# Transposes of softmax weights moved from the tensor engine to transposing DMAs in seven of eight attention passes

## The reference

```
q = heads(norm(x) @ Wq + bq);  k = heads(ctx @ Wk + bk);  v = heads(ctx @ Wv + bv)
attn = softmax(q k^T / sqrt(32))          # 128 x 2048 for each of 2 x 16 heads
out = (attn @ v) @ Wo + bo
```

## Time and profile before

| | us |
|---|---|
| median of 3 runs | 515.41 |
| the profiled execution | 515.1 |
| its span | 513.3 |
| PE busy | 495.2 |
| ACT busy | 266.2 |
| DVE busy | 307.7 |
| POOL busy | 42.2 |

### The profile page before, as it was taken

How to read it: one execution, slowest core, us unless ns; L and a number is a source line. 1 busy time by engine, 2 the same in 40 slices (tenths; PEclk the granted TensorE clock), 3 DMA queues, 4 the chain that set the end, 5 groups by cost and what they waited for, 6 DMA issues and landing times.

```text
span 513.3 us, 9255 instructions
## 1 busy us (share of the span) xinstructions
PE 495.2 (96%) x3742; PEld 378.2 (74%) x3742; DVE 307.7 (60%) x585; ACT 266.2 (52%) x401; POOL 42.2 (8%) x34
## 2 busy tenths in 40 slices
PE   8999998999999999999999999999899998999995
PEld 6786777777777777897877778757595866877663
DVE  3757532645554553346187384579379978975962
ACT  4230037495857641328357748467345727755730
POOL 0030000000199000000000000000002010000000
PEclk9999999999999999999999999999999999999999
DMA  8900000000341022220310000298387899876001
GB/s 277 357 2 1 1 1 0 2 1 1 108 162 64 1 77 89 82 83 1 106 39 3 0 3 0 68 421 334 109 324 271 316 390 377 298 298 240 1 0 41
DMA packets 11497, 63.52 MB, mean 124 GB/s; under 512 B 1600, under 2 KB 2112, under 8 KB 4544
## 3 DMA queue, kind: packets, MB, share of 16 engines
q1 hardware_dynamic: 11168, 62.67, 32.3%
q10 hardware_dynamic: 288, 0.27, 0.2%
HBM read 62.41 MB, written 0.52 MB: 123 GB/s over the span
## 4 chain that ended last, share of the span: by engine, by line
PE 83%; ACT 7%; DVE 5%; issue 4%; POOL 0%; POOLq 0%; ACTq 0%; DVEq 0%
PE ps L1155 36%; PE ps L1225 11%; PE ps L1239 6%; PE ps L1209 5%; ACT Pm L452 4%; PE ps L1471 3%; PE ps L1473 3%; PE ps L1472 3%; PE ps L1491 3%; PE ps L1430 1%; PE ps L1431 1%; PE ps L1432 1%; PE ps L1149 1%; PE ps L1420 1%; ACT PT L460 1%
## 5 line engine op out<-in xcount | busy, mean ns | idle before, releaser
L753 DVE TENSOR_SCALAR_CACHE_REDUCE Pm<-ps,small 128x512 f32<-128x512 f32 x96 | 66.4, 748 | 30.5 <-PE ps L1209 30.3
L460 ACT COPY PT<-ps 128x512 f32<-128x512 f32 x128 | 68.5, 592 | 28.9 <-PE ps L1225 28.9
L1225 PE MATMUL ps<-ident,Pm 128*128 128x128 f32 x512 | 69.3, 277 | 3.2 <-ACT Pm L452 3.2
L1225 PEld LDWEIGHTS ps<-ident,Pm 128*128 128x128 f32 x512 | 56.5, 141 | 18.0 <-issue 11.0
L452 ACT ACTIVATE Pm<-Pm,small 128x2048 f32<-128x2048 f32 x32 | 64.3, 2011 | 3.5 <-DVE Pm L753 3.5
L733 DVE SCALAR_TENSOR_TENSOR KrL<-ps,small,KrH 128x512 fp32r<-128x512 f32 x32 | 23.9, 747 | 61.2 <-ACT KrH L438 61.2
L1155 PE MATMUL ps<-wvH,ctxH 128*128 128x512 f32 x124 | 50.3, 405 | 1.0 <-DVE V L742 1.0
L1155 PE MATMUL ps<-ctxH,wkH 128*128 128x512 f32 x124 | 51.1, 412 | 0.0
L1155 PE MATMUL ps<-ctxL,wkH 128*128 128x512 f32 x124 | 48.6, 392 | 0.0
L1155 PE MATMUL ps<-ctxH,wkL 128*128 128x512 f32 x124 | 48.5, 391 | 0.0
L1155 PE MATMUL ps<-wvH,ctxL 128*128 128x512 f32 x124 | 48.4, 390 | 0.0
(11 more groups left out here) (229 smaller groups left out, 872.3 us busy)
## 6 DMA issues: line engine op xcount, KB each, us to landing
w1raw<-in_W SPq DMA_DIRECT2D x16, 1024.0 KB, 6.1
w2raw<-in_W SPq DMA_DIRECT2D x16, 1024.0 KB, 7.3
raw<-in_ctxT SPq DMA_DIRECT2D x7, 1024.0 KB, 5.2
woF<-in_ffn_Wo SPq DMA_DIRECT2D x4, 1024.0 KB, 10.0
wo<-in_wo SPq DMA_DIRECT2D x2, 1024.0 KB, 4.9
ctx_first<-in_ctxT SPq DMA_DIRECT2D x4, 256.0 KB, 4.7
wv_raw<-in_xWv SPq DMA_DIRECT2D x2, 512.0 KB, 8.2
wq<-in_xWq SPq DMA_DIRECT2D x1, 1024.0 KB, 13.3
```

The source lines that it names most:

```text
L460: act.copy(PT[:, c % 2, i, :, :].rearrange("p k t -> p (k t)"), ps[:, t_bank(p, c, i), :]).then_inc(pt_done, 1)
L753: dve.tensor_scalar(Pm[:, i, c * CH:(c + 1) * CH], ps[:, i, :], -1.0, mx[:, p % 2, i, c - 1:c] if c else NOT_YET, ALU.mult, ALU.min, accum ...
L1225: last = pe.transpose(ps[:, t_bank(p, c, i), j * P:(j + 1) * P], Pm[:, i, c * CH + j * P:c * CH + (j + 1) * P], ident[:])
```

## The change

For passes 0 to 6, chunks 2 and 3 of heads 0, 1 and 2 (six of the sixteen head chunks of a pass) are no longer turned by PE. A transposing DMA moves 2-byte elements, so an fp32 word is cut in its two 16-bit halves:

1. POOL copies the high halves and the low halves of a head's 1024 words into a staging buffer, in two copies (probs_split). The stage has two places for heads; it lies on the memory of PT slot 1. Head 2 waits for the DMA of head 0. All wait for value product 2 of the pass before, and in pass 4 for the self attention's products.
2. SP starts a transposing DMA of 128 x 2048 two-byte elements, 512 KB, from the stage back into Pm's chunks 2 and 3 of that head.
3. When all three DMAs of a pass have landed, ACT joins the halves of chunk 2 into PT in six copies of 512 elements, and POOL those of chunk 3 in six (probs_merged).

Chunk 2 now uses PT slot 1, and chunks 0, 1 and 3 all use slot 0, so the first copy of chunk 1 waits for value product 0. DVE's negations of chunks 2 and 3 wait for the joins. Value products 2 and 3 of a pass both stand early in the next loop. Keys 0 of passes 2, 3, 4, 6 and 7 are computed one loop earlier, ahead of scores 3. Batch 1's context is split by ACT (ctxH), POOL (ctxL 0 and 1) and DVE (ctxL 2 and 3, ahead and behind of KrL 2 in loop 4). Some semaphores of constants are joined in one.

```diff
+            def turned(p, i):                                   # SP
+                sp.wait_ge(p_split, 2 * (HD * p + i + 1))
+                sp.dma_start_transpose(Pm[:, i, PEC * CH:].bitcast(U16).rearrange("p (k t) -> p k t", t=T),
+                                       stage[:, i % 2, :, :, :].rearrange("p c h n -> p (c h n)")).then_inc(p_turned[i % 2], 16)
+            for p in range(G):
+                for i in range(HD):
+                    if p == G - 2 and i < 2:
+                        context_in(i)
+                    turned(p, i)
+                if p == G - 2:
+                    context_in(2)
+                    context_in(3)
...
+            def probs_split(p, i):                              # POOL
+                pool.wait_ge(exp_done, HPG * p + i + 1)
+                if p == G:
+                    pool.wait_ge(pv2_mm, 1)
+                if p:
+                    pool.wait_ge(pv_mm, C * (p - 1) + PEC + 1)
+                if i == 2:
+                    pool.wait_ge(p_turned[0], 16 * (2 * p + 1))
+                words = Pm[:, i, PEC * CH:].bitcast(U16).rearrange("p (c n h) -> p c n h", c=C - PEC, h=2)
+                for h in range(2):
+                    pool.tensor_copy(stage[:, i % 2, :, h, :], words[:, :, :, 1 - h]).then_inc(p_split, 1)
+            def probs_merged(p, c):                             # POOL; ACT's is alike
+                pool.wait_ge(p_turned[0], 16 * 2 * (p + 1))
+                pool.wait_ge(p_turned[1], 16 * (p + 1))
+                pool.wait_ge(pv_mm, slot_user(p, c))
+                for i in range(HD):
...
+                    for h in range(2):
+                        pool.tensor_copy(words[:, :, 1 - h], halves[:, h * CH:(h + 1) * CH]).then_inc(merged[c], 1)
...
             def probs_T(p, c, i):                               # ACT
-                if p * C + c >= 2:
-                    act.wait_ge(pv_mm, p * C + c - 1)
+                if slot_user(p, c) > 0:
+                    act.wait_ge(pv_mm, slot_user(p, c))
...
+                if p == G - 1:                                  # ACT, loop 3, behind chunk 0's copies
+                    context_high(0)
+                    context_high(1)
...
+                    if c == 2 and p < NP:
+                        probs_merged(p - 1, c)
+                    if p == G - 1 and c >= 2:
+                        context_high(c)
...
+                if p == G:                                      # DVE, loop 4
+                    context_low(2)
                 if p < NP:
                     keys(p, 2)
+                if p == G:
+                    context_low(3)
...
+                    probs_T(p - 1, 0, 0)                        # PE, loops 1 to 7
+                    probs_T(p - 1, 0, 1)
+                    keys(p, 2)
+                    probs_T(p - 1, 0, 2)
+                    probs_T(p - 1, 0, 3)
+                    scores(p, 0)
+                    probs_T(p - 1, 1, 0)
+                    probs_T(p - 1, 1, 1)
+                    weighted_values(p - 1, 0)
+                    probs_T(p - 1, 1, 2)
+                    probs_T(p - 1, 1, 3)
+                    scores(p, 1)
+                    keys(p, 3)
+                    probs_T(p - 1, 2, 3)
+                    weighted_values(p - 1, 1)
+                    if p == G + 3:
+                        masks(0)
+                    scores(p, 2)
+                    probs_T(p - 1, 3, 3)
+                    if early_keys(p + 1):
+                        keys(p + 1, 0)
+                    scores(p, 3)
```

More of the change, by code:

```diff
@@ L206, in perceiver_block @@
         NP = B * G
+        PEC = C // 2
+        HD = HPG - 1
+        PE_TURNS = HPG * PEC + (HPG - HD) * (C - PEC)
         NV = C * JT
@@ L238, in perceiver_block @@
         s_mm, s_done = sem("s_mm"), sem("s_done")
+        p_split, ctx_first1 = sem("p_split"), sem("ctx_first1")
+        merged = {PEC: sem("merged_act"), PEC + 1: sem("merged_pool")}
+        p_turned = [sem(f"p_turned{k}") for k in range(2)]
         exp_done, t_mm = sem("exp_done"), sem("t_mm")
@@ L312, in ffn_wo_in @@
                 sp.dma_start(woF[:, k, :], a["ffn_Wo"][:, k, :]).then_inc(woF_in, 16)
+            for p in range(G, NP - 1):
+                for i in range(HD):
+                    turned(p, i)
             sp.wait_ge(k_mm, NP * C)
@@ L567, in while_values, with probs_merged, context_high @@
                 values(1, n // JT, n % JT)
+            def probs_merged(p, c):
+                act.wait_ge(p_turned[0], 16 * 2 * (p + 1))
+                act.wait_ge(p_turned[1], 16 * (p + 1))
+                for i in range(HD):
+                    words = halves_of(PT[:, pt_slot(p, c), i, :, :].rearrange("p k t -> p (k t)"))
+                    halves = Pm[:, i, c * CH:(c + 1) * CH].bitcast(U16)
+                    for h in range(2):
+                        act.copy(words[:, :, 1 - h], halves[:, h * CH:(h + 1) * CH]).then_inc(merged[c], 1)
+            def context_high(c):
+                act.wait_ge(raw_in[c], 32 if c else 16)
+                act.copy(ctxH[c][:], raw[c][:]).then_inc(ctx_hi1, 1)
             for p in range(1, NP + 1):
@@ L985, in first_split_here, with context_low @@
                 first_low(t)
+            def context_low(c):
+                dve.wait_ge(ctx_hi1, c + 1)
+                dve.tensor_tensor(ctxL[c][:], raw[c][:], ctxH[c][:].bitcast(F32), ALU.subtract).then_inc(ctx_split1, 1)
             def alongside(p, at_point):
@@ L1160, in keys @@
                 b, g = divmod(p, G)
-                if b:
-                    pe.wait_ge(ctx_split1, c + 1)
+                if b and c < 2:
+                    pe.wait_ge(ctx_first1, c + 1)
+                elif b:
+                    pe.wait_ge(ctx_split1, c - 1)
                 else:
@@ L1492, in ffn_out, with early_keys @@
                 last.then_inc(f_mm, 1)
+            def early_keys(p):
+                return 1 < p < NP and p != G + 1
             for p in range(1, NP + 1):
@@ L1499, in _ @@
                     first_experts(0)
-                if more:
+                if more and not early_keys(p):
                     keys(p, 0)
                 if late:
+                    weighted_values(p - 2, C - 2)
                     weighted_values(p - 2, C - 1)
```

131 lines of the change are left out of this document (79 added, 52 removed).

## The result

The changed kernel takes **532.3 us** (median of 4 runs, 530.6 to 532.3) against 515.4 (515.3 to 515.6): ratio 1.032, 95% interval 1.030 to 1.034. Its profiled execution has a span of 530.4 us, 17.1 above that of before. The forecast was 519.8: the sign was right, the loss nearly four times as large as said.

What follows compares the result with a forecast made beforehand. It took ACT to set the end of each loop's head and PE alone to bound the tail. Its loop terms summed to +4.4 us on the median of 515.4, giving 519.8 us, range 512.5 to 540.

Steps and rivals of the forecast that it cites:

- ACT's head is the same chain of work: Middle loop, scores 3 to scores 0: ACT sets the end, so scores 0 still starts at 12.95 us.
- The wait for PT slot 0: Each loop: chunk 1's first copy waits for value product 0, so PE waits before the third turn; 0.75 us.
- The DMAs, priced 4.5 us: Transposing DMAs land before ACT's join even strictly in order, 3 us in hand, late only above 5.6 us each.
- rival (a): DMAs late, so joins, negations and scores 3 wait; some 538 us at 6.5 us each, 555 at 7.3; chance 0.2.
- Loop 3's casts on ACT: Two casts of 1.90 us make ACT 1.6 late, a fourth delays exp 0 of loop 4 about 0.8; +2.4.
- Neither sets the end: Middle loop: neither ACT's join with DVE's negations nor POOL's join sets the loop's end; 0.25 us gained a loop.
- keys 0 out and a value product in: Loop 6's head, longer on PE: this exchange is worth 1.9 us; with the tail -2.15.
- keys 2 waited for ctxL 2: Loop 4: DVE makes ctxL 2 only after KrL 1 and outputs, so keys 2 start 4.4 us later.
- scores 3 then waits for DVE's chunk 2, so that only 0.4 comes back: Loop 4: no early keys 0, but scores 3 waits for DVE's negations; -0.4 within the loop's +3.85.
- masks stand ahead of ACT's join: Loop 7's tail: no early keys, but scores 3 waits for the join behind the masks; net 0.
- Value product 2 ahead of the reciprocals: Loop 8: ACT already waits 1.01 us for PE's reciprocals, and value product 2 goes in front; +1.0.
- (b): Loops 3 and 4: the context's hand-over costs nothing, 2.4 and 4.5 fall away; 512.9 us or 507.6; chance 0.2.

Runs made afterwards that it cites:

- run 1: Changed kernel with dummy matmuls on TensorE, 26 ahead of keys 2 of loop 4 and 12 ahead of scores 3 in loops 4 and 7: 527.1 us.
- Run 3: Changed kernel with the joins exchanged, GpSimd joining chunk 2 and ScalarE chunk 3 ahead of its last copy: 528.6 us.
- run 2: Changed kernel with VectorE's subtractions for ctxL 2 and ctxL 3 one gap earlier in loop 4: 527.1 us.
- run 4: Changed kernel with both the earlier ctxL 2 and 3 subtractions and the exchanged joins: 522.3 us.
- run 6: The kernel of run 4 with 12 dummy matmuls on TensorE ahead of scores 3 in loops 4 and 7: 520.3 us.
- run 8: Changed kernel with joins exchanged, context casts and GpSimd's queue rearranged, keys 0 back in the loop's head, value product 2 ahead of scores 3: 516.1 us.
- run 10: The kernel of run 8 with exponentials 1 and 3 earlier, value product 0 directly behind scores 0, contexts 2 and 3 loaded later and VectorE's context work reordered: 507.5 us.
- run 11: The kernel of run 10 with context 1's load also behind the third transposing DMA of its loop: 508.5 us.

## Why the prediction was right, and where it was wrong

The shift of the changed kernel against before, from the ends of scores 3 in the two timelines of PE (104.25 and 104.91 in loop 1, 131.88 and 132.90, 159.51 and 162.20, 187.14 and 197.98, 278.78 and 293.45, 309.30 and 323.49, 339.07 and 354.39) and the spans. The last column is the same for run 1's profiled execution, in which the clock doesn't fall; what it has less than the column beside it is the price of the falls:

| stretch | forecast | measured | with run 1's dummies |
|---|---|---|---|
| loop 1, loop 2 | -0.25, -0.25 | +0.7, +0.4 | +0.9, +0.4 |
| loop 3 | +2.15 | +1.7 | +1.7 |
| loop 4 | +3.85 | +8.2 | +5.6 |
| values' section and loop 5 | +0.75 | +3.8 | +1.7 |
| loop 6 | -2.15 | -0.5 | -0.5 |
| loop 7 | -0.7 | +1.1 | +0.5 |
| loop 8 and rest | +1.0 | +1.8 | -0.4 |
| sum | +4.4 | +17.1 | +9.8 |

(Rounded terms; loop 1 has what stood ahead of it.)

**Right.** Line 1225's turns come 344 times. "ACT's head is the same chain of work" held: from exp 0 to scores 0 of loop 2 the changed kernel takes 11.0 us (105.52 to 116.50), against 11.1 in the earlier trace rows. The wait for PT slot 0, priced 0.75, is 0.85 in each loop but loop 3, where it is 2.1 behind the casts. The DMAs, priced 4.5 us, took 4.5, and no join waited for one; rival (a) falls with that. The slack was larger than the text's 3 us, which had the three DMAs strictly one behind the other: in loop 2 the third has landed 5.5 us before ACT's join. Loop 3's casts on ACT were priced well: loop 3 is 1.3 us longer than loop 2, and exp 0 of loop 4 comes 1.0 later behind scores 3 than in loop 3, against 1.6 and 0.8. The Trainium skill's 261 GB/s for a transposing DMA ("DMA: Bandwidth & Descriptors", "Latency and other measured facts") and its 2 us of fixed cost gave an estimate of 4.0; the trace has 4.5, and 9.3 at most beside a load. GpSimd's copy of 1024 two-byte elements takes 1.04 us, against 1.02.

**Wrong, the steady loop.** The step that failed is "Neither sets the end". Its term was ACT's six copies of 512 at 0.5 each from 22.7 to 25.7, and "DVE's negations of chunk 2 then end near 27.2, just as scores 3 wants its last bank". A copy is 0.655, and the sum left no margin: the join took 3.93, DVE ended 4.2 us behind scores 2, scores 3 took 1.94 and not 0.97, and exp 0 of the next pass came as much later. Run 3 put it right: 27.22 us, 0.8 below the changed kernel. That is 0.6 to 0.9 a loop in loops 1 and 2. Scores 3 are stretched in the same way in loops 3, 5 and 6 (1.96, 2.17 and 1.95 us). In loop 6, from scores 0 to the end of scores 3, it is 1.0 of the 1.65 that the forecast lacks; the other 0.65 is the head, where keys 0 out and a value product in were worth 1.25 and not 1.9.

**Wrong, loop 4.** The mechanism was right: keys 2 waited for ctxL 2, 5.58 us against "some 4". The term itself was 1.5 us short (keys 2 start 5.9 later than before, counted from the start of scores 3, against 4.4): DVE's KrL 1, behind which ctxL 2 stands, comes 10.96 us behind the start of scores 3 and not 9.39 as before, with scores 3 stretched by the join and exp 0 behind the fourth cast. More of what the sum lacked stands behind it. One part is the clock, for which no term stood in it: before it had not fallen in any loop, and I took every duration as fixed. The falls at this wait, at scores 3 of loop 4 and at scores 3 of loop 7 cost 7.3 us together by the last column (loop 1 came 0.2 longer in that execution): 2.5 in loop 4, 2.2 in the values' section and loop 5 (the two value products alone take 3.64 in place of 2.0), 0.6 in loop 7 and 2.2 in what follows it. The other is scores 3 of loop 4: "scores 3 then waits for DVE's chunk 2, so that only 0.4 comes back" had those negations at 0.67 each; they came at 1.25.

**Wrong, loop 7.** The text saw that masks stand ahead of ACT's join and that scores 3 wait for it, and set this at 0 against the early keys that this loop lacks. Scores 3 wait 1.91, 0.39 and 0.44 us, the clock is at 0.50 for 10 us from there, and from scores 0 to the end of scores 3 the loop takes 19.2 us where it took 17.1 before: +2.1 and not 0.

**Wrong, loop 8.** Value product 2 ahead of the reciprocals was to cost 1.0. With the clock whole, loop 8 and the rest together are 0.4 us shorter than before; what the changed kernel has beyond that, 2.2, goes with the fall that begins in loop 7. Where the 1.0 is made up was not looked at.

**The rivals.** (b), that the hand-over costs nothing, did not happen, but its place was named rightly: with ctxL 2 in the gap of 3.96 us keys 2 began 1.0 us behind the turns, and 5.1 us came back (run 2; the text priced this part at 4.5, and at 6.9 together with loop 3's casts, which run 2 leaves). The Trainium skill's "Who interferes with whom" ("SBUF — State Buffer") was left outside the sum as up to 1 us on DVE. Here the lockout fell on the other side: DVE's ctxL 2 took its usual 2.28, and GpSimd's split of head 2, at 172.76, took 3.80 for two copies that take 2.03 otherwise:

```profile
172.76 3.80 POOL L451 COPY stage<-Pm 128x1024 uint16<-128x1024 uint16 x2 [2.23 <-DMA Pm<-stage]
```

**The account.** The loss beyond the forecast was 12.5 us (532.3 less 519.8). By the profiled executions 7.3 of it are the clock's falls, for which the sum had no term. The rest is in the waits: ACT's join, which paces scores 3, and what keys 2 of loop 4 and scores 3 of loops 4 and 7 wait beyond their terms, less the 1.4 us by which loop 8 and the rest came out better. The two ctxL ahead and the joins exchanged gave back 10.0, of which some 2 are the clock's by the estimate in run 4, and the dummies another 2.0: 520.3 us. That this lies half a microsecond from the forecast is luck: loop 3 of that kernel (run 6) is 2.7 us and loop 6 2.4 us longer than before, with a fall in each, where the forecast had +2.15 and -2.15. How the gains of runs 2 and 3 divide exactly between clock and waits stays open.

## What to carry to other kernels

Work taken off the bounding engine comes back only if the engine has something to do in the time: the DMAs took the turns off TensorE in the kernel that lost 17 us and in the one that gained 8, and the difference is the order in the queues, with the casts of two context chunks moved from ScalarE to VectorE. When a step moves to another engine, price its rate as well as its sum, since a consumer that goes head by head runs at the producer's pace; and put the piece that is wanted first on the engine that is free first. Give each new idle of several microseconds on TensorE a second term, for the clock behind it, and for its size take about six tenths of (1 - clock) x time, which is what came back here twice between profiled executions (7.3 of 11.9 with run 1, 2.2 of 3.4 between runs 4 and 6). Before a median is compared with a profile, look at the clock of each execution: the falls that were gone in run 1's profile were not gone in its other three.

## What the runs showed of the hardware

- The granted clock went to 1.2 GHz after idles of TensorE, for some 3 to 10 us each: in and behind a wait of 5.58 us, but also behind waits of 0.57 to 0.75 us within scores. In run 8 waits of 0.15 to 0.18 at the same place led to it in one loop of seven. No run shows which idle is enough. (The Trainium skill, "TensorE: Matmul & The Clock Gate", "HAM oscillation — how this bites in real kernels", counts the penalty of a throttled stretch as its length times one half; by that rule this kernel's is the 11.9 us, and what taking the falls away gave is 7.3. The measurement decides.)
- VectorE and GpSimd hold each other up, either way. VectorE's cast of 128x2048 took 1.22 us alone, and 5.07 beside GpSimd's subtraction for ctxL 1, behind whose end it ended by 1.1 us (run 10, DVE's timeline); its subtraction took 3.01 beside GpSimd's split copies, where it takes 2.29 alone:

```profile
156.29 5.07 DVE L1095 CAST ctxH<-raw 128x2048 fp32r<-128x2048 f32 x1
161.40 3.01 DVE L1104 TENSOR_TENSOR ctxL<-raw,ctxH 128x2048 fp32r<-128x2048 f32 x1
```

- A transposing DMA of 512 KB that lands in 4.5 us took 9.1 where a 1 MB load had been issued 0.6 us ahead of it (run 10; 9.3 with one 1.1 us ahead in the changed kernel), and 6.6 with one right behind it (run 11). Issuing the one of 9.1 us took 5.4 us of SP's queue, where 1.9 is the median, so the next was issued late.
- A copy of 512 two-byte elements with a stride is 0.655 us on ScalarE (3.93 for six) and 0.70 on GpSimd (4.17 for six): half the bytes of the 512 floats that ScalarE copies from PSUM in 0.54 (1.07 to 1.09 for two), and no faster.
